# MLP up-projection: the last 32 columns of both matrices as one 128-column weight, moved one block ahead, and y's low part moved in VectorE's queue

## The reference

```python
y = y @ out_proj_w.T + u
zm = rmsnorm(y, post_norm_w)
mlp = jax.nn.gelu(zm @ l1_w.T) * (zm @ l2_w.T) @ l3_w.T
return y + mlp
```

## Time and profile before

| | us |
|---|---|
| median of 3 runs (1076.63 to 1077.24) | 1076.65 |
| the profiled execution | 1076.75 |
| its span | 1075.0 |
| PE busy in the span | 1050.8 |
| DVE busy | 877.8 |
| ACT busy | 710.8 |

### The profile page before, as it was taken

The page is one execution under the profiler, slowest core; times in us unless marked ns, Lnnn a source line. Parts: engine busy times, 40 slices in busy tenths (PEclk is TensorE's granted clock), DMA queues, the critical chain, the costliest instruction groups (busy, mean ns, idle before and its releaser), DMA issues.

```text
span 1075.0 us, 24951 instructions
## 1 busy us (share of the span) xinstructions
PE 1050.8 (98%) x9012; PEld 1008.5 (94%) x9012; DVE 877.8 (82%) x2322; ACT 710.8 (66%) x1589; POOL 299.5 (28%) x575
## 2 busy tenths in 40 slices
PE   8899999999999999999999999999999999999998
PEld 7777888899989999999999999989999999999997
DVE  7999998774788888888887878897888888887776
ACT  7879887764456666666666666656666666666644
POOL 7677775470101112111111111111112111111111
PEclk9999999999999999999999999999999999999999
DMA  3337977986322222233222222432222223222000
GB/s 130 120 117 236 294 216 196 363 318 151 83 66 41 54 57 50 52 52 58 59 60 58 52 51 60 122 96 41 60 51 50 52 53 59 59 58 60 21 21 31
DMA packets 112491, 102.83 MB, mean 96 GB/s; under 512 B 7552, under 2 KB 103744, under 8 KB 112112
## 3 DMA queue, kind: packets, MB, share of 16 engines
q1 hardware_dynamic: 111136, 98.67, 36.2%
q0 software_dynamic: 736, 2.51, 0.6%
q10 hardware_dynamic: 496, 0.05, 0.0%
HBM read 75.75 MB, written 30.70 MB: 99 GB/s over the span
## 4 chain that ended last, share of the span: by engine, by line
PE 67%; DVE 6%; issue 2%; ACT 1%; POOL 0%; POOLq 0%; DVEq 0%; ACTq 0%
PE ps_ring L1551 35%; PE ps_w L1551 16%; PE ps_m L1551 9%; PE ps_o L1551 4%; PE ps_rt L1566 2%; DVE base L1373 1%; PE ps_w L1561 1%; DVE bn L1277 1%; PE ps_m L1617 1%; DVE prod L1320 0%; DVE ht_l L1289 0%; DVE pt_l L1289 0%; POOL sc L1129 0%; ACT rows L1254 0%; DVE yrow L1512 0%
## 5 line engine op out<-in xcount | busy, mean ns | idle before, releaser
L1129 POOL TENSOR_TENSOR sc<-sc,small 128x2 f32<-128x2 f32 x127 | 94.5, 744 | 676.8 <-DVE sc L1501 404.6
L1194 ACT ACTIVATE gate<-ps_ring 128x256 f32<-128x256 f32 x192 | 73.0, 381 | 129.7 <-PE ps_ring L1551 128.9
L1215 ACT ACTIVATE hid<-ps_ring,small 128x256 f32<-128x256 f32 x256 | 112.1, 483 | 24.2 <-PE ps_w L1551 13.4
L1551 PE MATMUL ps_ring<-mt_l,wl_h 128*128 128x256 f32 x640 | 125.5, 277 | 2.6 <-DVE mt_l L1289 2.6
L1551 PE MATMUL ps_ring<-mt_h,wl_h 128*128 128x256 f32 x640 | 125.5, 277 | 1.8 <-DVE prod L1320 1.3
L1551 PE MATMUL ps_ring<-mt_h,wl_l 128*128 128x256 f32 x640 | 124.9, 277 | 0.0
L1289 DVE TENSOR_TENSOR ht_l<-hid,ht_h 128x256 fp32r<-128x256 f32 x256 | 103.1, 423 | 16.5 <-ACT ht_h L1219 10.6
L1551 PE MATMUL ps_ring<-xt_h,we_h 128*128 128x256 f32 x512 | 104.8, 285 | 2.5 <-DVE prod L1320 2.4
L1551 PE MATMUL ps_ring<-xt_h,we_l 128*128 128x256 f32 x512 | 101.3, 279 | 0.0
L1551 PE MATMUL ps_ring<-xt_l,we_h 128*128 128x256 f32 x512 | 101.3, 279 | 0.0
L1320 DVE TENSOR_TENSOR prod<-ps_ring,gate 128x256 f32<-128x256 f32 x192 | 80.7, 420 | 24.2 <-ACT gate L1194 20.6
(11 more groups left out here) (203 smaller groups left out, 2720.2 us busy)
## 6 DMA issues: line engine op xcount, KB each, us to landing
toep_scratch<-taps_scratch SPq DMA_DIRECT2D x26, 512.0 KB, 7.4
toep<-toep_scratch SPq DMA_DIRECT2D x26, 512.0 KB, 8.8
xa<-in_x SPq DMA_DIRECT2D x16, 512.0 KB, 4.9
x_scratch<-x2c SPq DMA_DIRECT2D x16, 512.0 KB, 3.7
x2s<-x_scratch SPq DMA_DIRECT2D x32, 256.0 KB, 6.7
xa_c<-in_x SPq DMA_DIRECT2D x32, 256.0 KB, 2.7
xb_c<-in_x SPq DMA_DIRECT2D x32, 256.0 KB, 2.7
yin<-seq SPq DMA_DIRECT2D x124, 64.0 KB, 5.5
```

What stands on the lines that cost most here:

```text
L1129: nc.gpsimd.tensor_tensor(sc[:, to], sc[:, to], neg_half[:, 0, 0:CC], ALU.pow).then_inc(S[done], 1)
L1194: nc.scalar.activation(gate[rows_of, m % 2], ring[m % RING][rows_of, 0], ACT.Gelu_apprx_tanh).then_inc(S["gate_done"], 1)
L1215: nc.scalar.activation(hid[:, m % HIDS], block_of, ACT.Gelu, bias=b1s[:, m:m + 1]).then_inc(S["hid_done"], 1)
L1551: mm = nc.tensor.matmul(out, lhs(a, kk), rhs(b, kk), start=(j == 0), stop=(closed and j == len(todo) - 1))
```

## The change

- `wrest` becomes one tile of 128 columns: the high parts of the 32 l2 and 32 l1 columns, then the low parts of both. Phase B writes the same numbers to the new places.
- The rest becomes block 4 of six (`REST_AT = FB - 2`) and the fifth full block becomes block 5. The rest takes four matmuls: two with all 128 columns on the high part of the input, which give high x high in partitions 0 to 63 and low weight x high input in 64 to 127, and two with 64 columns on the low part of the input.
- The two halves have to be added now. ACT copies partitions 64 to 127 from PSUM to SBUF (`rest_low`), DVE adds them to partitions 0 to 63 (`rest_sum`, `rest_done`), and ACT takes the GELU of the sum. ACT does `product_high` of block 3 between its copy and that GELU. DVE does `product_low` of block 3 between the sum and the rest's product.
- The high parts of blocks 4 and 5 are made on DVE as before, now the rest's first and then the full block's.
- Where an FFN unit is there (`h` valid), y's low part is no longer ahead of block 4's product but behind `hidden_low(h, 1)`.

The core of the diff:

```diff
-        wrest = [sb(whole, f"wrest_{s}", [P, KB, 2 * REST], F32R) for s in "hl"]
+        wrest = sb(whole, "wrest", [P, KB, 4 * REST], F32R)
...
+    REST_AT = FB - 2
...
             def mlp_gate(n, m):
                 act.wait_ge(S["ml_mm"], FB * n + m + 1)
                 wait(act, S["prod_done"], FB * n + m - 1)
-                rows_of = slice(0, P) if m < FULL else slice(REST, 2 * REST)
-                nc.scalar.activation(gate[rows_of, m % 2], ring[m % RING][rows_of, 0],
-                                     ACT.Gelu_apprx_tanh).then_inc(S["gate_done"], 1)
+                opened, source = gate[:, m % 2], ring[m % RING][:, 0]
+                if m == REST_AT:
+                    nc.scalar.activation(opened[2 * REST:], source[2 * REST:], ACT.Copy).then_inc(S["rest_low"], 1)
+                    product_high(n, m - 1)
+                    act.wait_ge(S["rest_done"], n + 1)
+                    opened = source = opened[REST:2 * REST]
+                nc.scalar.activation(opened, source, ACT.Gelu_apprx_tanh).then_inc(S["gate_done"], 1)
...
-                        if 0 < m < FB - 1:
+                        if 0 < m < REST_AT:
                             product_high(n, m - 1)
...
             def mlp_product(n, m):
                 b = FB * n + m
+                wait(dve, S["pl_done"], b - 1)
+                if m == REST_AT:
+                    rest_sum(n)
+                    product_low(n, m - 1)
                 dve.wait_ge(S["gate_done"], b + 1)
-                wait(dve, S["pl_done"], b - 1)
-                if m < FULL:
+                if m != REST_AT:
                     value, gated = ring[m % RING][:, 1], gate[:, m % 2]
                 else:
-                    value, gated = ring[m % RING][0:REST, 0], gate[REST:2 * REST, m % 2]
+                    value, gated = gate[0:REST, m % 2], gate[REST:2 * REST, m % 2]
                 nc.vector.tensor_tensor(product_views(m)[1], value, gated, ALU.mult
                                         ).then_inc(S["prod_done"], 1)
-                if m > 0:
+                if 0 < m != REST_AT:
                     product_low(n, m - 1)
                 if m == FB - 1:
                     product_low(n, m)
+
+            def rest_sum(n):
+
+                pair = gate[:, REST_AT % 2]
+                dve.wait_ge(S["rest_low"], n + 1)
+                nc.vector.tensor_tensor(pair[0:2 * REST], ring[REST_AT % RING][0:2 * REST, 0], pair[2 * REST:], ALU.add
+                                        ).then_inc(S["rest_done"], 1)
...
-                if valid(n + 1, UC):
+                if valid(n + 1, UC) and not valid(h, UC):
                     gate_y(n + 1, 2)
...
                     for m in range(HB):
                         hidden_low(h, m)
+                        if m == 1 and valid(n + 1, UC):
+                            gate_y(n + 1, 2)
...
                 else:
-                    mm = product(bank[0:2 * REST, 0], lambda a, kk: wrest[a][:, kk],
-                                 lambda b, kk: zt[b][:, kk], KB)
+                    for b, columns in enumerate((4 * REST, 2 * REST)):
+                        for kk in range(KB):
+                            mm = nc.tensor.matmul(bank[0:columns, 0], wrest[:, kk, 0:columns], zt[b][:, kk],
+                                                  start=(b == kk == 0), stop=(b == kk == 1),
+                                                  skip_group_check=True)
                 mm.then_inc(S["ml_mm"], 1)
```

More of the change, by code:

```diff
@@ L752, in _ @@
                 parts = ((raw[:, k, :, 0:FULL * P], [w[:] for w in dst]),
-                         (raw[:, k, :, FULL * P:], [w[:, :, at:at + REST] for w in wrest]))
+                         (raw[:, k, :, FULL * P:], [wrest[:, :, i:i + REST] for i in (at, 2 * REST + at)]))
                 for piece, (high, low) in parts:
@@ L1009, in phase_c @@
                    xhat_done yrow_done
-                   squared rms_arg rms_done zm_done zt_mm zh_done zl_done ml_mm gate_done prod_done
+                   squared rms_arg rms_done zm_done zt_mm zh_done zl_done ml_mm rest_low rest_done gate_done prod_done
                    ph_done high_here pl_done stacked m_mm a_done a_stat a_var a_scale a_mean x1_done x_stat x_var
@@ L1030, in piece, with full_block @@
                     for w in (base2[:], we2[0][:], we2[1][:])]
+        def full_block(m):
+            return m - (m > REST_AT)
         def product_views(m):
-            if m < FULL:
-                return pt[0][:, m], prod[:, m % 2], pt[1][:, m]
+            if m != REST_AT:
+                return pt[0][:, full_block(m)], prod[:, m % 2], pt[1][:, full_block(m)]
             return pstack[0:REST], prod[0:REST, m % 2], pstack[2 * REST:]
@@ L1334, in product_low @@
                     dve.wait_ge(S["high_here"], (FB - ACT_HIGHS) * n + m - ACT_HIGHS + 1)
-                if m == FULL:
+                if m == REST_AT:
                     nc.vector.tensor_copy(pstack[REST:2 * REST], src).then_inc(S["stacked"], 1)
@@ L1577, in mlp_block @@
                 bank = ring[m % RING]
-                if m < FULL:
+                if m != REST_AT:
                     for side, w in enumerate((wl1, wl2)):
-                        mm = product(bank[:, side], lambda a, kk: w[a][:, kk, m * P:(m + 1) * P],
+                        mm = product(bank[:, side], lambda a, kk: w[a][:, kk, chunk(full_block(m))],
                                      lambda b, kk: zt[b][:, kk], KB, passes=PASSES_T,
```

## The result

The changed kernel takes 1084.26 us (median of 4 runs, 1083.31 to 1085.42), the kernel before 1076.68 beside it: a ratio of 1.0063, 95% interval 1.0044 to 1.0081. It is slower by 7.6 us; the forecast was 1076.3, with 1072.8 to 1080.3. The profiled execution took 1084.11 us, its span 1082.4.

The account below looks back on a forecast made before the run. PE was taken to bound steps 4 to 16, 20 to 30 and 31, the DVE chain steps 0 to 3 and 17 to 19. Gain 4.5 less losses 4.1 gave 0.4 us faster, 1076.3 us; range 1072.8 to 1080.3.

Parts of the forecast that it names:

- 25 x 0.18 = 4.5 us of gain: PE-bound steps: two matmuls fewer save 0.227 us each, less a possible PE wait; 0.18 kept per step, bounds 3.2 and 5.7.
- The wait at the FFN's fifth block: PE waits there for ACT's `hid` to free the bank: up to 0.10 us in each PE-bound step, or not at all.
- The 0.37 by which ACT is later: PE-bound step: ACT's table load starts at 654.79 instead of 654.42, or only 0.27 later if instructions overlap.
- my lower bound: PE-bound steps: the lower end of the gain, 0.13 us a step, 3.2 us in all.
- The pace: Rival on the FFN's first product, 5.66 or 5.45 us: turned in every step, 5.2 us either way; chance 0.07 faster, 0.05 slower.
- The losses: Steps 0 to 3 and 17 to 19, mostly DVE-bound, get longer by 4.1 us together, bounds 2.3 and 4.9.
- `yt_l` behind the FFN's second group has cover: PE-bound step: the moved `yt_l` ends near 659.2, some 0.5 us before PE needs it.
- the cover of `yrow`: PE-bound step: `yrow` and the normalised rows come 0.95 us later; their cover falls from 1.8 to 0.7 us and holds.

Follow-up runs that it names:

- two_less: The kernel before without the rest's two low weight x high input matmuls, part of the output left out: 1070.70 us, ratio 0.9943.
- yl_alone: The kernel before with only y's low part moved behind the FFN's second low part: 1077.05 us, ratio 1.0003.
- yl_back: The changed kernel with y's low part back at its old place ahead of block 4's product: 1087.11 us, ratio 1.0095.
- order_narrow_t: order_alone plus one discarded matmul with a 64-column weight ahead of turn_second's transposes: 1085.07 us, ratio 1.0073.
- order_alone: The kernel before with the rest as block 4 of six, six matmuls, no copy or sum, `yt_l` in its old place: 1084.23 us, ratio 1.0070.

## Why the prediction was wrong

- **"25 x 0.18 = 4.5 us of gain"** is the step that failed. The 0.227 us for two narrow matmuls in it holds (*two_less*, 5.65 us in all). What it takes off, a wait of some 0.05 at one place with PE's pace unchanged, does not: the 24 steps lost 3.1 us where this term has 4.3 of gain for them, through 4.28 us of longer gaps and 4.05 of slower pace.
- *The wait at the FFN's fifth block*, taken as 0.05 with 0.10 as the worst, measured 0.10 on the mean of 22 steps (4.28 us of longer gaps, less 2.06 in steps 12 and 29, over 22). The place and mechanism were right, the size was that of the bound. The 0.37 by which ACT is later had the lost overlap in it, but I doubted it and took the middle. The trace has it at each change of partitions: `last_norm` to copy 656.31 + 0.59 to 656.93, copy to high part 0.40, GELU to full gate 658.30 - 657.86 = 0.44. ACT is 0.52 later, and the 0.15 more are small things: the sum starts 0.10 behind the copy's end (657.41) instead of 0.04, each instruction 0.02 to 0.03 behind the one before, and the 32-partition GELU takes 0.42, not 0.37. A wait of 0.10 alone would have left 0.127 us a step, 3.2 in all, my lower bound.
- *The pace.* I had it among the rivals, "if the change turns it over in every step it is 25 x 0.21", at 0.05 for the slower side. It cost 4.05 us in steps 4 to 16 and 20 to 30. That this is near the rival's price is luck: it thought of the FFN's 48 matmuls, which were slow already in 22 steps and changed little in number (steps 4 and 20 no longer have theirs at the fast pace, but two of the eight blocks have it in nearly every third step); the slow pace grew behind them, over `ps_o`, `ps_m` and, one step in three, the MLP. Its price for a turn was wrong as well: step 20 has 0.21 us less in the FFN, but `ps_o` and `ps_m` are slow behind it, and the whole step takes 24.47 us, 0.07 less than the others. The chance of 0.05 for a thing marked "I don't know what sets it", in a kernel whose steps all stand on one pattern, was the real error.
- *POOL's long pair*, 1.0 us in each of steps 12 and 29, stood in no case. The cover of `last_norm` was never costed, since ACT seemed to have time.
- *The losses*, forecast / measured: step 0 0.45 / 0.79, step 1 0.2 / 0.43, step 2 0.95 / 1.16, step 3 0.3 / 0.44, step 17 0.95 / 0.88, step 18 0.95 / 1.15, step 19 0.3 / 0.15. Together 4.1 / 5.0, just over the bound of 4.9. Some 0.2 of step 2's 1.16 are the stretch at clock 0.50, so that step's own loss is the 0.95 of the forecast. Step 18 takes 27.0 to 27.9 us in the traces of the kernels with the old order and no sum, so tenths say little there; its order went as written, the sum and both GELUs ahead of the table load.
- *`yt_l` behind the FFN's second group has cover* held: *yl_alone* is within 0.1% of the kernel before. So did the cover of `yrow`: no long gap stands ahead of `ps_o` or of the second transposes in the 24 steps.

The sum by the measured terms: 24 PE-bound steps 5.45 less, gaps 4.28 and pace 4.05 more; the other steps 5.0 more; 7.9. The stages have 0.3 us more than these counts find, and 0.8 less stands ahead of step 0 and from step 31 on, which gives the span's 7.4; the medians have 7.6.

What stays open is what chooses the pace. Shown is that it has two levels at one clock, that the same instructions run at either (steps 4 and 5 of the kernel before), that other engines are as busy at either (DVE at 95% and 97% of the FFN in steps 4 and 5), that the order of the blocks changes it where two matmuls fewer do not, that one matmul more ahead of the transposes restores it in the new order, and that neither waits (satisfied ones, moved or added) nor the width of the last weights decide it as I thought. What stays open too is why POOL's pair is long; all that is shown is where it stands and the packet ahead of it.

## What to carry to other kernels

A PE-bound loop has a pattern of its own, and its steps are worth counting by the distance between matmul starts before a matmul is taken out: here 48 matmuls fewer gave back 5.45 us and the slower pace, which the order alone brings too, took 4.05. When an edit both saves matmuls and moves blocks, time the move by itself first. A matmul saved at the price of a sum elsewhere isn't free: here the sum on DVE and ACT cost 5.5 us of time for the 5.65 that PE saved.

## What the runs showed of the hardware

- PE runs fp32r matmuls of 256 columns at 113.3 or at 117.6 ns each, both at a granted clock of 1.00, and stays at one for dozens of matmuls. A lasting change comes within two or three matmuls of a place where a product begins, a weight changes its shape, or PE has waited (*yl_back*, step 8: the FFN's first 23 matmuls at the fast pace, a wait of 0.4 us, the rest at the slow one), not in the middle of equal matmuls. The instructions don't fix it: in the kernel before, the FFN's 48 matmuls are slow in 22 of the 24 PE-bound steps, and in steps 4 and 20 none is (the earlier trace rows has step 20).
- The wide load costs nothing: the rest's four matmuls, two with 128 columns of weights and two with 64, take 0.45 us, 0.113 each (655.69 to 656.14 in the chain of the changed kernel's step 16).
- ACT: an instruction whose partitions start elsewhere than the last one's starts when that has ended (658.30 behind 657.86 + 0.42), in both directions; with the same partitions it starts 0.28 us behind one of 0.38.
- The three operations of POOL on `shift` (128 x 2 elements), 0.19 to 0.53 us as a rule, take 0.65 to 1.5 in single cases, and in the same steps in every trace of kernels of one kind: step 18 in all 19, steps 12 and 29 with the sum, step 23 with the new order alone.
- In stretches with a granted clock of 0.50 (1.2 GHz; five of the traces have one) the distance of matmuls is 213 ns (213, 213, 214 in turn). Half of it, 106.7, is less than either pace at clock 1.00, so both have something on top, 6.6 and 10.9 ns, if the rest goes with the clock.
- In the one execution of 2124.24 us (*order_narrow_t*) the median distance of matmuls was 223 ns from its start to its end, against 116 in *order_alone*, while ACT and DVE kept their lengths. This trace holds no record of the clock, so the 1.00 that its windows print says nothing. 223 is near the 213 of the stretches at clock 0.50, so a clock at that level throughout is likely and not shown. The three executions after it were normal. I don't know why.
